# Twelve groups instead of six get their senders by edge number, ScalarE issues the dense stores, and results follow 13 steps behind instead of 17

## The chip, the cores and the metric

One core of a Trainium2 chip runs the whole kernel. The metric is the device time of one execution in microseconds (us). TensorE (PE), VectorE (DVE), ScalarE (ACT), GpSimd (POOL) and SyncE (SP) each work through their own instruction list in order and wait on semaphores; DMAs are issued from SP, POOL and, after the change, ACT. Work on SP is only the issuing of DMAs.

## The reference, cut to what matters

```python
# x: 100000 x 128, E = 25000 edges; edge_index = stack([src, dst]), so src is the receiver
recv, send = (edge_index[0], edge_index[1])
f = concatenate([h[recv], h[send], rel_pos, distance], -1)      # 25000 x 260
s = silu(silu(f @ W1 + b1) @ W2 + b2) @ W3 + b3                 # one score per edge
p = exp(s - segment_max(s, recv)[recv])
alpha = p / (segment_sum(p, recv)[recv] + EPS)
msg = h[send] @ Wv * (alpha * node_weight[send])[:, None]
out = layernorm(x + (h + segment_sum(msg, recv)))               # over 128 features
```

Every one of the 100000 rows is normalized; only rows that receive an edge also get a sum of messages.

## The kernel before, in words

The edges are first sorted by receiver (VectorE, up to about 110 us). From there two kinds of work run side by side.

**Dense work.** The 100000 rows are cut into 98 blocks of 1024 (128 partitions by 8 rows). A block is loaded into one of `X_RING` = 8 places of `xin` (`load_block`, line 323), gets its statistics on DVE (`dense_stats`, line 969), a chain of 11 small DVE instructions for four blocks at once turns them into scale and bias (`drs`, up to line 951), and it is scaled in place: 7 of its 8 rows by ACT (`norm`, line 510), one by DVE (`dense_norm`, line 990). SP stores it (`store_block`, line 332). The place is free for block j+8 when that store has landed. The statistics of blocks 2i and 2i+1 belong to turn i, and their scaling to turn i+2.

**Edge work.** The sorted edges make 49 groups of 512. For each group POOL gathers the receivers' rows (`hk`, four indirect DMAs of 128 rows) and the senders' rows (`rec`, four more). The numbers of the senders and the edge features must be brought into sorted order first. For 43 groups this is a *lookup*: one-hot rows on DVE, 24 products on PE (`look`, line 713), a selection on DVE (`take_places`), and four small products (`words`, line 700). For the other six groups (`TAKEN`: 4, 12, ..., 44) POOL gathers number and features from HBM by edge number (`rt`, four indirect DMAs a group, issued ahead of the first `rec`). POOL's list is: `hk` of four groups, all `rt`, then `rec` of group g and `hk` of group g+4 in turn, the last `rec` groups alone, `hk` of groups 39 to 48 (their place in SBUF holds the lookups' tables until then), and at last the scatters of the 49 groups' results (line 447). The scatters begin when SP has seen the last dense store land.

A gathered `rec` group is in one of `HS_RING` = 4 places; SP writes it to HBM (`write_rec`, line 347), which frees the place for group g+4 of the ring, and SP loads it later into `region` (`load_rec`, line 353).

**Turns and steps.** All engines follow one list, `TURNS`. A *step* s is one beat of the edge pipeline: transposes of group s, first layer of s-1, second of s-2, scores of s-3, weighted sums of s-10 (`Z_LAG`), their product with Wv one step later, statistics at s-12 (`Y_LAG`) and the scaled results (`res`, ACT line 559) 17 steps behind. Every fourth step holds the softmax of a batch of four groups. A step has three parts. A *turn* i holds lookup i (while there are lookups), dense pair i, and parts of steps: none in turns 0 to 9, one part in each of turns 10 to 42, and from turn 43 a whole step (turn 43 is step 11). There are 67 steps and 99 turns, of which the last dense statistics fall into turn 48.

SP's list in a turn is: store of a block, the load for the next lookup, `write_rec`, the loads of a step (each with a wait: for z, for y, for the weights of two groups before), a load of a block, a store, a load. Where it waits, everything behind it waits. `write_rec` of group g stands in turn looks(g) - 1 + 7, where looks(g) counts the lookups up to g; a group that is `TAKEN` so shares its turn with a neighbour.

Of the kernel before, what the change touches and what calls it, by code (L numbers as in the profile page):

```python
# [12 lines left out]
P = 128  # L13
# [23 lines left out]
Y_LAG, Z_LAG, M_LAG, KROW_LAG = 12, 10, 9, 8  # L37
LAST_STEP = 67
# [6 lines left out]
REC_LAG = 7  # L45
E_FROM = 10
PARTS = 3
FIRST_TAKEN, TAKEN_STEP = 4, 8
# [26 lines left out]
def turn_plan():  # L75

    plan, left, turn = [], [(s, p) for s in range(LAST_STEP) for p in range(PARTS)], 0
    while left:
        now = []
        if E_FROM <= turn < LOOKS:  # L80
            now.append(left.pop(0))
        elif turn >= LOOKS:
            now.append(left.pop(0))
            while left and left[0][0] == now[0][0]:
                now.append(left.pop(0))
        plan.append(now)
        turn += 1
    return plan
# [5 lines left out]
def looks(g):  # L94

    return sum(1 for v in LOOKED if v <= g)

# [16 lines left out]
def gnn_kernel(nc, x, xw, rec5, snd_tab, ef_tab, rcv_nat, id_nat, signs, iota, rowid, colid, word, w16d, w1, b1, w2, b2, w3, b3,  # L114
# [11 lines left out]
    with ExitStack() as ctx:  # L126
# [171 lines left out]
        def chain_turn(b):  # L298
            return batch_end(b) + Y_LAG + 1

        def res_turn(g):
            return max(chain_turn(batch_of(g)) + 1 + g % BATCH, g + Y_LAG + BATCH + 1)
# [3 lines left out]
        def _(sp):  # L306
# [18 lines left out]

            def store_block(j):
                if 0 <= j < NB:
                    wait(sp, "norm_a", j + 1)
                    wait(sp, "norm_d", j + 1)
                    if j == NB - 1:  # L330
                        wait_ring(sp, stored, j - 1, 16)
                    sp.dma_start(out[rows_of(j), :].rearrange("(p r) h -> p r h", p=P), xin[:, j % X_RING]
                                 ).then_inc(stored[j % X_RING], 16)
# [53 lines left out]
            for i, now in enumerate(TURNS):  # L387
                store_block(2 * (i - 3) + 1)
                if i + 1 < LOOKS:
                    load_places(i + 1)  # L390
                for g in range(G):
                    if looks(g) - 1 + REC_LAG == i:
                        write_rec(g)
# [19 lines left out]
                store_block(2 * (i - 2))  # L413
# [89 lines left out]
        def _(act):  # L503
            def norm(i, half):
                j = 2 * (i - 2) + half
                if 0 <= j < NB:
                    wait(act, "chain_d", (j // 4 + 1) * STEPS)
                    for n in range(ACT_ROWS):
# [17 lines left out]
            def hidden(s):  # L526
# [7 lines left out]
                for b in range(NBATCH):  # L534
                    if batch_end(b) + 4 == s:
# [4 lines left out]
            def results(s):  # L540
                g = s - Z_LAG
# [4 lines left out]
                for b in range(NBATCH):  # L546
                    if batch_end(b) + 5 == s:
                        n = group_tiles(b)
                        wait(act, "alphaT_done", b + 1)
                        wait(act, "acol_ready", b - 1)  # L550
                        nc.scalar.activation(alT[:, b % 2, 0:n], bank[6][:, 0:n], ACT.Copy).then_inc(S["alT_ready"], 1)
# [27 lines left out]
        def _(pe):  # L579
# [79 lines left out]
            def small_turns(s):  # L659
# [6 lines left out]
                for b in range(NBATCH):  # L666
                    if batch_end(b) + 5 == s:
# [23 lines left out]
            def turns(s):  # L691
                if s + 1 < G:
                    turn_rows(s + 1)
                    turn_senders(s + 1, sum(batch_end(b) + 5 <= s for b in range(NBATCH)))
# [46 lines left out]
        def _(dve):  # L741
# [220 lines left out]
            def dense_stats(i):  # L962
# [10 lines left out]
                if i % 2 == 1 or i == NPAIR - 1:  # L973
# [3 lines left out]
                    def gate():  # L977
                        wait(dve, "norm_a", 4 * (k - 1))
                        wait(dve, "norm_d", 4 * (k - 1))
# [4 lines left out]
            def dense_norm(i):  # L984
                for j in (2 * (i - 2), 2 * (i - 2) + 1):
                    if 0 <= j < NB:
                        wait(dve, "chain_d", (j // 4 + 1) * STEPS)
                        for n in range(ACT_ROWS, BR):
# [103 lines left out]
            def part_two(s):  # L1092
                for b in range(NBATCH):
                    if chain_turn(b) == s:
                        def gate(b=b):
# [3 lines left out]
                                             "chain_e", b * STEPS, gate))  # L1099
                    if batch_end(b) + 4 == s:  # L1100
                        softmax_first(b)
                    if batch_end(b) + 6 == s:
# [6 lines left out]

            def part_three(s):  # L1110
# [3 lines left out]
                for b in range(NBATCH):  # L1114
                    if batch_end(b) + 4 == s:
                        softmax_second(b)
                more(99)
                if s == batch_end(NBATCH - 1) + 5:
                    dve.sem_inc(S["parts_ready"], 1)

            for i, now in enumerate(TURNS):
# [3 lines left out]
                for b in range(NBATCH):  # L1125
                    if (batch_end(b) + 4, 0) in now:
                        take_scores(b)
# [119 lines left out]
```

## Time and profile before

| | |
|---|---|
| median of 3 runs | 1012.76 us (1011.95 to 1016.06) |
| profiled execution, its time | 1010.98 us |
| its span in the trace | 1009.2 us |
| PE / DVE / ACT / POOL busy | 735.5 / 655.5 / 527.1 / 596.9 us |
| moved by DMA | 188.47 MB |
| lookups on PE | 110.3 to 560.2 us |
| last step on PE | 955 us |
| last scatter issued | 1007.5 us |

The span runs from the first to the last instruction; 1.8 us of the execution's time lie around it. An engine's busy time is a mean over stages that differ: sort (to 110 us), lookups without steps, lookups with a third of a step, whole steps with dense work (to about 663 us), whole steps alone, and an end in which only POOL has much to do.

### The profile page before, as it was taken

Reading aid. Unit: us, or ns where it says so; the run is one execution under the profiler, and the core shown is the slowest. Engines: PE = TensorE matmul, PEld = TensorE weight load, DVE = VectorE, ACT = ScalarE, POOL = GpSimd, SP = SyncE. Lnnn points to the kernel's source line nnn. Section 1 sums busy time; section 2 is a strip of 40 time slices with the busy share of each in tenths; the row PEclk is TensorE's granted clock in tenths of the full one; section 3 lists DMA queues with packets and bytes.
Section 4 is the critical chain, followed back from the end, with each engine's and each line's share of the span. In section 5 each row is a group of like instructions: output and inputs, shape, how many; then the busy total and the mean of one; then the engine's idle time right before and its main releaser. Section 6 shows DMA issues by size and latency. Waiting matters only on the chain.

```text
span 1009.2 us, 13449 instructions
## 1 busy us (share of the span) xinstructions
PE 735.5 (73%) x3718; PEld 493.6 (49%) x3718; DVE 655.5 (65%) x2314; ACT 527.1 (52%) x1230; POOL 596.9 (59%) x624
## 2 busy tenths in 40 slices
PE   0001688889878878797889786799999999996700
PEld 0000355555555545564556454566766666665600
DVE  8988789877766757676787666544355535547741
ACT  0000066566555645555556576876566666664630
POOL 3000777777777777777774337717644444446677
PEclk9999988989987878888898988899999999998755
DMA  6000369999889979979999869533322222222131
GB/s 215 0 0 5 78 186 315 336 344 344 288 269 320 327 217 331 329 223 291 356 321 321 247 208 304 168 117 101 92 80 83 80 83 85 83 65 66 65 80 45
DMA packets 120371, 188.47 MB, mean 187 GB/s; under 512 B 21147, under 2 KB 80182, under 8 KB 120296
## 3 DMA queue, kind: packets, MB, share of 16 engines
q1 hardware_dynamic: 100648, 148.85, 45.5%
q0 software_dynamic: 19648, 38.74, 13.8%
q8 instruction: 31, 0.51, 0.2%
q14 instruction: 44, 0.36, 0.1%
HBM read 109.89 MB, written 77.76 MB: 186 GB/s over the span
## 4 chain that ended last, share of the span: by engine, by line
PE 41%; DVE 19%; POOL 15%; issue 8%; DMA 8%; ACT 6%; SPq 2%; POOLq 0%; DVEq 0%; ACTq 0%
PE bank L713 9%; POOL rec L443 6%; POOL hk L443 6%; PE bank L680 4%; PE bank L687 4%; PE bank L643 4%; PE bank L655 4%; PE bank L634 3%; DMA xin<-in_x 3%; POOL out_rows L447 3%; PE bank L652 3%; PE bank L653 3%; ACT xin L510 3%; DVE region L776 3%; PE bank L700 2%
## 5 line engine op out<-in xcount | busy, mean ns | idle before, releaser
L510 ACT ACTIVATE xin<-xin,drs 128x128 f32<-128x128 f32 x686 | 269.4, 480 | 268.8 <-DVE drs L951 268.8
L447 POOL DMA_INDIRECT out_rows<-hk,sidx_t x196 | 192.4, 982 | 155.6 <-ACT hk L559 83.8
L713 PE MATMUL bank<-hk 128*125 128x512 bf16 x1032 | 267.5, 422 | 8.3 <-DVE snd_i L1026 5.4
L443 POOL DMA_INDIRECT hk<-in_x,kg_t x196 | 186.4, 951 | 143.5 <-DVE kg_t L860 84.0
L443 POOL DMA_INDIRECT rec<-in_xw,snd_i x196 | 185.5, 947 | 96.3 <-issue 56.7
L713 PEld LDWEIGHTS bank<-hk 128*125 128x125 bf16 x1032 | 156.7, 154 | 115.1 <-issue 40.6
L969 DVE BATCH_NORM_STATS2 dst<-xin 128x6 f32<-128x256 f32 x392 | 135.6, 413 | 32.8 <-DMA xin<-in_x 32.5
L1011 DVE TENSOR_SCALAR hk<-hk,rid 128x512 bf16<-128x512 f16 x344 | 110.0, 381 | 0.5 <-DMA hk<-vc_d 0.3
L1078 DVE TENSOR_TENSOR hk<-bank,hk 128x512 f32<-128x512 f32 x49 | 33.6, 687 | 102.1 <-PE bank L680 102.1
L700 PE MATMUL bank<-wsel,hk 125*128 125x5 f32 x344 | 52.4, 276 | 59.1 <-DVE hk L1018 59.1
L700 PEld LDWEIGHTS bank<-wsel,hk 125*128 125x128 f32 x344 | 48.6, 218 | 73.2 <-DVE hk L1018 71.7
L559 ACT ACTIVATE hk<-hk,ers 128x128 f32<-128x128 f32 x196 | 79.5, 482 | 0.4 <-DVE ers L951 0.4
L530 ACT ACTIVATE x<-bank,bcol 128x512 f32<-128x512 f32 x49 | 33.6, 686 | 66.5 <-PE bank L655 66.5
L586 PE MATMUL bank<-ident,region 128*128 128x128 f32 x8 | 2.7, 445 | 86.8 <-DVEq L792 86.8
L655 PEld LDWEIGHTS bank<-efT,w 16*128 16x128 f32 x392 | 47.2, 186 | 37.2 <-issue 37.2
L680 PE MATMUL bank<-wvh,zs 128*128 128x128 f32 x392 | 59.6, 300 | 6.8 <-ACT zs L545 3.4
L545 ACT ACTIVATE zs<-bank 128x512 f32<-128x512 f32 x49 | 29.0, 591 | 64.7 <-PE bank L687 64.7
L1069 DVE TENSOR_SCALAR m_q<-krow,kcol,acol 128x128 f32<-128x128 bf16 x196 | 57.1, 348 | 7.4 <-DMA krow<-seg_d 6.4
L1018 DVE SCALAR_TENSOR_TENSOR hk<-hk,cid,bank 125x512 f32<-125x512 f16 x43 | 31.9, 742 | 44.7 <-PE bank L713 44.7
L643 PE MATMUL bank<-x,w2s 128*128 128x512 f32 x98 | 60.9, 706 | 0.0
L687 PE MATMUL bank<-m_q,region 128*128 128x128 f32 x392 | 57.8, 296 | 0.0
L680 PEld LDWEIGHTS bank<-wvh,zs 128*128 128x128 f32 x392 | 52.6, 208 | 9.6 <-ACT zs L545 6.0
(203 smaller groups left out, 1020.7 us busy)
## 6 DMA issues: line engine op xcount, KB each, us to landing
xin<-in_x SPq DMA_DIRECT2D x98, 512.0 KB, 6.8
out_rows<-xin SPq DMA_DIRECT2D x98, 512.0 KB, 7.5
rec_d<-rec SPq DMA_DIRECT2D x49, 258.0 KB, 5.6
region<-rec_d SPq DMA_DIRECT2D x49, 258.0 KB, 3.4
hk<-vc_d SPq DMA_DIRECT2D x43, 256.0 KB
krow<-seg_d SPq DMA_DIRECT2D x49, 128.0 KB, 3.3
hk<-in_x,kg_t POOLq DMA_INDIRECT x196, 5.5
rec<-in_xw,snd_i POOLq DMA_INDIRECT x196, 6.0
```

What stands on the lines that cost most here:

```text
L443: pool.indirect_dma_start(out=to, out_offset=None, in_=frm, in_offset=bass.IndirectOffsetOnAxis(ap=index, axis=0)).then_inc(done, 16)
L447: pool.indirect_dma_start(out=out, out_offset=bass.IndirectOffsetOnAxis(ap=index, axis=0), in_=frm, in_offset=None).then_inc(done, 16)
L510: ins = nc.scalar.activation(xin[:, j % X_RING, n, :], xin[:, j % X_RING, n, :], ACT.Identity, bias=drs[:, j // 4 % 2, 1, c:c + 1], scale= ...
L559: ins = nc.scalar.activation(hk[:, g, q, :], hk[:, g, q, :], ACT.Identity, scale=ers[:, b % 2, 0, n:n + 1], bias=ers[:, b % 2, 1, n:n + 1])
L643: pe.matmul(bank[2][:], w2s[:], x1[:], start=True, stop=True).then_inc(S["mm2_done"], 1)
L655: ins = pe.matmul(bank[1][:, q * P:(q + 1) * P], w16[:, q, :], efT[:, g % 2, :], start=False, stop=(q == TPG - 1), skip_group_check=True)
L680: ins = pe.matmul(bank[4][:, q * P:(q + 1) * P], zs[:, q * P:(q + 1) * P], wvh[:], start=True, stop=True)
L687: ins = pe.matmul(bank[5][:, q * P:(q + 1) * P], rr[:, g % R_RING, q, 0:H], m_q[:, g % 2, q, :], start=True, stop=True)
L700: ins = pe.matmul(bank[7][:, q * WORDS:(q + 1) * WORDS], sel[0:SEL, q * P:(q + 1) * P], wsel[0:SEL, :], start=True, stop=True)
L713: ins = pe.matmul(bank[7][0:SEL, :], tab[:, k, n, 0:SEL], oh[:, k, :], start=(k == 0 and n == 0), stop=(k == CH - 1 and n == PIECES - 1))
L969: ins = vec.bn_stats(dst[:, c:c + 2, :].rearrange("p j w -> p (j w)"), xin[:, j % X_RING, n:n + 2, :].rearrange("p j h -> p h j"))
L1011: ins = vec.tensor_scalar(pair(oh[:, k, :]), vt[:, u % 2, :, 0, :], rid[:, k:k + 1], None, ALU.is_equal)
```

## The change

- `TAKEN_STEP` goes from 8 to 4: twelve groups (4, 8, ..., 48) take their numbers by `rt`, and 37 lookups are left.
- `E_FROM` goes from 10 to 11, and while there are lookups every third turn holds two parts: 4/9 of a step a turn. Turn 37 holds the last two parts of step 11, turn 38 is step 12, turn 51 is step 25. There are 60 steps and 86 turns.
- `write_rec` of group g stands in turn g + 9, one in each turn, behind the step's loads and the first block load, and `HS_RING` is 6.
- The stores of the dense blocks go from SP to ACT: one behind `norm(i, 0)`, one behind the step's parts. `norm_d` is waited for only where DVE has a share.
- ACT scales all 8 rows of a block in turns before 37 (`act_rows`), 5 of 8 after; DVE the other 3.
- The lags: sums 8 steps behind, weights 7, statistics 10, results 13; softmax one step earlier, and its transposed weights are copied and used within one step.

```diff
-HS_RING, R_RING, X_RING = 4, 12, 8
+HS_RING, R_RING, X_RING = 6, 12, 8
-ACT_ROWS = 7
-Y_LAG, Z_LAG, M_LAG, KROW_LAG = 12, 10, 9, 8
-LAST_STEP = 67
+Y_LAG, Z_LAG, M_LAG, KROW_LAG = 10, 8, 7, 6
+LAST_STEP = 60
-REC_LAG = 7
-E_FROM = 10
+REC_LAG = 9
+E_FROM = 11
-FIRST_TAKEN, TAKEN_STEP = 4, 8
+FIRST_TAKEN, TAKEN_STEP = 4, 4
...
         if E_FROM <= turn < LOOKS:
             now.append(left.pop(0))
+            if (turn - E_FROM) % PARTS == PARTS - 1:
+                now.append(left.pop(0))
...
+def act_rows(j):
+    return BR if j // 2 + 2 < LOOKS else 5
...
+            return batch_end(b) + Y_LAG
-            return max(chain_turn(batch_of(g)) + 1 + g % BATCH, g + Y_LAG + BATCH + 1)
+            return chain_turn(batch_of(g)) + (g % BATCH if batch_of(g) < NBATCH - 2 else 0)
...
-                store_block(2 * (i - 3) + 1)
-                for g in range(G):
-                    if looks(g) - 1 + REC_LAG == i:
-                        write_rec(g)
...
-                store_block(2 * (i - 2))
+                if 0 <= i - REC_LAG < G:
+                    write_rec(i - REC_LAG)
...
+            def store(j):
+                if 0 <= j < NB:
+                    wait(act, "norm_a", j + 1)
+                    wait(act, "norm_d", shared(j))
+                    if j == NB - 1:
+                        wait_ring(act, stored, j - 1, 16)
+                    act.dma_start(out[rows_of(j), :].rearrange("(p r) h -> p r h", p=P), xin[:, j % X_RING]
+                                  ).then_inc(stored[j % X_RING], 16)
...
                 norm(i, 0)
+                store(2 * (i - 3) + 1)
                 for s, part in now:
                     (turned, hidden, results)[part](s)
+                store(2 * (i - 2))
                 norm(i, 1)
```

**POOL, around its first `rec` gather** (`rt` are the numbers by edge number, each row a run of indirect DMAs). Before:

```order
13 L443 DMA hk<-in_x,kg_t 128x128 x16
14 L443 DMA rt<-in_rec,idx_t 128x5 x24
15 L443 DMA rec<-in_xw,snd_i 128x129 x4
16 L443 DMA hk<-in_x,kg_t 128x128 x4
17 L443 DMA rec<-in_xw,snd_i 128x129 x4
```

After:

```order
13 L442 DMA hk<-in_x,kg_t 128x128 x16
14 L442 DMA rt<-in_rec,idx_t 128x5 x48
15 L442 DMA rec<-in_xw,snd_i 128x129 x4
16 L442 DMA hk<-in_x,kg_t 128x128 x4
17 L442 DMA rec<-in_xw,snd_i 128x129 x4
```

Twenty-four more gathers stand ahead of the first senders' rows; the rest of POOL's list is as it was.

**SP, at the write-back of group 42** (`out_rows<-xin` is a dense store, `rec_d<-rec` a write-back, `region<-rec_d`, `yf_d`, `yl_d` and `krow` are a step's loads and stores, `far` and `cont` those of a softmax). Before, from the write-back of group 42 (turn 44) to those of 43 and 44 (turn 45):

```order
291 L347 DMA rec_d<-rec 128x4x129
292 L353 DMA region<-rec_d 128x4x129
293 L377 DMA krow<-seg_d 128x512
294 L360 DMA far<-far_d 16x129
295 L361 DMA cont<-cont_d 16x128
296 L323 DMA xin<-in_x 128x1024
297 L332 DMA out_rows<-xin 128x1024
298 L323 DMA xin<-in_x 128x1024
299 L332 DMA out_rows<-xin 128x1024
300 L347 DMA rec_d<-rec 128x4x129 x2
```

After, from the write-back of group 41 (turn 50) to that of group 42 (turn 51):

```order
270 L349 DMA rec_d<-rec 128x4x129
271 L355 DMA region<-rec_d 128x4x129
272 L386 DMA yf_d<-hk 1x512
273 L386 DMA yl_d<-hk 1x512
274 L379 DMA krow<-seg_d 128x512
275 L349 DMA rec_d<-rec 128x4x129
```

The stores are gone from SP, there is one write-back a turn, and that of group 42 has moved from turn 44 to turn 51, behind the loads of step 25.

**ACT, in the lookups with parts of steps** (`xin` are the rows of dense blocks, the others belong to the step's parts). Before:

```order
72 L510 ACTIVATE xin<-xin,drs 128x128 x14
73 L530 ACTIVATE x<-bank,bcol 128x512
74 L533 ACTIVATE efT<-bank 16x128
75 L510 ACTIVATE xin<-xin,drs 128x128 x28
76 L518 ACTIVATE hkT<-bank 128x512
```

After:

```order
58 L509 ACTIVATE xin<-xin,drs 128x128 x16
59 L568 DMA out_rows<-xin 128x1024
60 L529 ACTIVATE x<-bank,bcol 128x512
61 L532 ACTIVATE efT<-bank 16x128
62 L568 DMA out_rows<-xin 128x1024
63 L509 ACTIVATE xin<-xin,drs 128x128 x16
64 L568 DMA out_rows<-xin 128x1024
```

Each run of scaled rows is longer by a seventh, and two stores a turn now stand in ACT's list.

## Rows read from the trace of the kernel before

**Rows 1.** Stretches (us): length, busy time by engine, PE clock, DMA share, GB/s.
```profile
208.20:295.80 87.60, 76.81 (x352) 49.50 (x353) 65.83 (x228) 53.78 (x134) 66.27 (x71) 0.90 0.95 320
560.20:641.00 80.80, 56.89 (x302) 39.52 (x302) 55.10 (x191) 51.84 (x119) 41.73 (x44) 0.83 0.78 230
641.00:905.00 264.00, 251.28 (x1495) 174.66 (x1494) 122.13 (x404) 177.26 (x376) 134.41 (x137) 0.99 0.33 95
```

**Rows 2.** Timeline of PE, the products of lookups 0, 9, 19 and 42.
```profile
110.31 8.00 PE L713 MATMUL bank<-hk 128*125 128x512 bf16 x24 [2.74 <-DVE hk L1011]
192.01 5.39 PE L713 MATMUL bank<-hk 128*125 128x512 bf16 x24 [0.34 <-DVE snd_i L1026]
290.49 5.34 PE L713 MATMUL bank<-hk 128*125 128x512 bf16 x24
553.83 6.41 PE L713 MATMUL bank<-hk 128*125 128x512 bf16 x24
```

**Rows 3.** Timeline of POOL: start, length, indirect DMA, idle before it.
```profile
119.82 0.94 POOL L443 DMA_INDIRECT rt<-in_rec,idx_t  x1 [0.30 <-issue]
149.81 0.95 POOL L443 DMA_INDIRECT rec<-in_xw,snd_i  x1 [0.30 <-issue]
500.60 0.94 POOL L443 DMA_INDIRECT rec<-in_xw,snd_i  x1 [0.30 <-issue]
607.18 1.02 POOL L443 DMA_INDIRECT hk<-in_x,kg_t  x1 [0.31 <-issue]
677.83 1.00 POOL L447 DMA_INDIRECT out_rows<-hk,sidx_t  x1 [20.83 <-SPq L419]
1005.24 1.00 POOL L451 DMA_INDIRECT out_rows<-xin,fixi  x1 [0.30 <-issue]
```

**Rows 4.** Page, part 5: the scatters of the results.
```profile
L447 POOL DMA_INDIRECT out_rows<-hk,sidx_t x196 | 192.4, 982 | 155.6 <-ACT hk L559 83.8
```

**Rows 5.** Waits of SP's own queue over the whole span.
```profile
SPq L347 <- DMA rec<-in_xw,snd_i: 132.1, 31, 8.6
SPq L332 <- ACT xin L510: 61.7, 25, 10.5
```

**Rows 6.** Timelines of SP and of POOL, from 573 us.
```profile
573.27 0.43 SPq L347 DMA_DIRECT2D rec_d<-rec  x1
591.68 1.39 SPq L347 DMA_DIRECT2D rec_d<-rec  x2
...
578.98 0.94 POOL L443 DMA_INDIRECT rec<-in_xw,snd_i  x1 [9.09 <-DMA rec_d<-rec]
597.16 0.94 POOL L443 DMA_INDIRECT rec<-in_xw,snd_i  x1 [13.50 <-DMA rec_d<-rec]
```

**Rows 7.** Timelines of DVE and of SP, blocks 24 to 33.
```profile
223.75 2.40 DVE L969 BATCH_NORM_STATS2 dst<-xin 128x6 f32<-128x256 f32 x7
260.98 2.75 DVE L969 BATCH_NORM_STATS2 dst<-xin 128x6 f32<-128x256 f32 x8
...
246.07 0.34 SPq L332 DMA_DIRECT2D out_rows<-xin  x1
253.23 0.33 SPq L323 DMA_DIRECT2D xin<-in_x  x1
```

**Rows 8.** Line 332, the dense store: ns per issue, least/median/most.
```profile
L332 SPq DMA_DIRECT2D out_rows<-xin x98: 337/394/1785, 131.2 to 663.2; - x98
```

**Rows 9.** Groups of ACT from 560.2 to 641 us, and one timeline row.
```profile
L510 ACT ACTIVATE xin<-xin,drs 128x128 f32<-128x128 f32 x76 | 30.0, 481 | 9.2 <-DVE drs L951 9.2
...
906.13 1.64 ACT L559 ACTIVATE hk<-hk,ers 128x128 f32<-128x128 f32 x4
```

**Rows 10.** Timeline of PE: the sums of groups 11 and 38.
```profile
683.02 1.06 PE L687 MATMUL bank<-m_q,region 128*128 128x128 f32 x8
...
903.87 1.67 PE L687 MATMUL bank<-m_q,region 128*128 128x128 f32 x8
```

**Rows 11.** Timeline of ACT after a step with a softmax.
```profile
627.81 2.42 ACT L510 ACTIVATE xin<-xin,drs 128x128 f32<-128x128 f32 x6 [4.71 <-DVE drs L951]
```

More of the change, by code:

```diff
@@ L96, in looks, with shared @@
     return sum(1 for v in LOOKED if v <= g)
+def act_rows(j):
+    return BR if j // 2 + 2 < LOOKS else 5
+def shared(j):
+    return sum(1 for k in range(j + 1) if act_rows(k) < BR)
 def pool_plan():
@@ L298, in chain_turn @@
         def chain_turn(b):
-            return batch_end(b) + Y_LAG + 1
+            return batch_end(b) + Y_LAG
         def res_turn(g):
-            return max(chain_turn(batch_of(g)) + 1 + g % BATCH, g + Y_LAG + BATCH + 1)
+            return chain_turn(batch_of(g)) + (g % BATCH if batch_of(g) < NBATCH - 2 else 0)
         @block.sync
@@ L324, in load_block @@
                                  ).then_inc(x_in[j % X_RING], 16)
[L326 to L333, printed above, removed]
             for j in range(X_RING):
@@ L507, in norm @@
                     wait(act, "chain_d", (j // 4 + 1) * STEPS)
-                    for n in range(ACT_ROWS):
+                    for n in range(act_rows(j)):
                         c = j % 4 * BR + n
@@ L534, in hidden @@
                 for b in range(NBATCH):
-                    if batch_end(b) + 4 == s:
+                    if batch_end(b) + 3 == s:
                         n = group_tiles(b)
@@ L540, in results @@
             def results(s):
+                for b in range(NBATCH):
+                    if batch_end(b) + 4 == s:
+                        n = group_tiles(b)
+                        wait(act, "alphaT_done", b + 1)
+                        wait(act, "acol_ready", b - 1)
+                        nc.scalar.activation(alT[:, b % 2, 0:n], bank[6][:, 0:n], ACT.Copy).then_inc(S["alT_ready"], 1)
                 g = s - Z_LAG
@@ L545, in results @@
                     nc.scalar.activation(zs[:], bank[5][:], ACT.Copy).then_inc(S["zs_ready"], 1)
[L546 to L551, printed above, removed]
                 for g in range(G):
@@ L666, in small_turns @@
                 for b in range(NBATCH):
-                    if batch_end(b) + 5 == s:
+                    if batch_end(b) + 4 == s:
                         n = group_tiles(b)
@@ L693, in turns @@
                     turn_rows(s + 1)
-                    turn_senders(s + 1, sum(batch_end(b) + 5 <= s for b in range(NBATCH)))
+                    turn_senders(s + 1, sum(batch_end(b) + 4 <= s for b in range(NBATCH)))
             def words(u):
@@ L978, in gate @@
                         wait(dve, "norm_a", 4 * (k - 1))
-                        wait(dve, "norm_d", 4 * (k - 1))
+                        wait(dve, "norm_d", shared(4 * (k - 1) - 1))
                     n = (2 * i + 2 - 4 * k) * BR
@@ L985, in dense_norm @@
                 for j in (2 * (i - 2), 2 * (i - 2) + 1):
-                    if 0 <= j < NB:
+                    if 0 <= j < NB and act_rows(j) < BR:
                         wait(dve, "chain_d", (j // 4 + 1) * STEPS)
-                        for n in range(ACT_ROWS, BR):
+                        for n in range(act_rows(j), BR):
                             c = j % 4 * BR + n
@@ L1099, in part_two, with part_three @@
                                              "chain_e", b * STEPS, gate))
+                    if batch_end(b) + 3 == s:
+                        take_scores(b)
+                        softmax_first(b)
+            def part_three(s):
+                for b in range(NBATCH):
                     if batch_end(b) + 4 == s:
-                        softmax_first(b)
-                    if batch_end(b) + 6 == s:
                         wait(dve, "alT_ready", b + 1)
@@ L1108, in part_two @@
                         dve.wait_ge(S["acol_ready"], b + 1)
-            def part_three(s):
                 if 0 <= s - M_LAG < G:
@@ L1114, in part_three @@
                 for b in range(NBATCH):
-                    if batch_end(b) + 4 == s:
+                    if batch_end(b) + 3 == s:
                         softmax_second(b)
                 more(99)
-                if s == batch_end(NBATCH - 1) + 5:
+                if s == batch_end(NBATCH - 1) + 3:
                     dve.sem_inc(S["parts_ready"], 1)
@@ L1124, in _ @@
                 one_hot(i, 0, EARLY)
-                for b in range(NBATCH):
-                    if (batch_end(b) + 4, 0) in now:
-                        take_scores(b)
                 if 0 <= i - 1 < LOOKS:
```

## The prediction

> **What bounds the kernel now.** I first cut the span at PE's lookups. A lookup's 24 products stand in one row; a turn begins where the products of the lookup before end. Lookup 0 ends at 118.3 us, lookup 9 at 197.4, lookup 19 at 295.8, lookup 42 at 560.2 [rows 2]. So turns 1 to 9 take 8.79 us each (79.1 / 9), turns 10 to 42 11.0 us, of these the first ten 9.84 and the last 23 11.5 (264.4 / 23). The same work gets slower from about turn 20. POOL says why: it issues an indirect DMA every 1.25 us (24 `rt` gathers from 119.82 to 149.81), so that `rec` of g and `hk` of g+4 take 10.02 us together: group 35 starts at 500.60, (500.60 - 149.81) / 35 [rows 3]. 49 groups fall on 43 lookup turns, and 10.02 x 49 / 43 = 11.4 us a turn. SP carries this to the others: its largest wait but one is that of `write_rec` for POOL's gather, 132.1 us, and behind it stand the dense loads [rows 5]. So turns 20 to 42 go at POOL's pace. Those before are held elsewhere: DMA is 95% busy at 320 GB/s and PE 76.8 of 87.6 us [rows 1].
>
> From 560.2 to 641 us six turns hold a whole step and dense work, 13.5 us each, though PE is busy 56.9 of 80.8 us [rows 1]: ACT waits for `drs`, which DVE finishes late behind a softmax (4.7 us at 627.81 [rows 11]), and SP's stores wait for ACT (61.7 us in all [rows 5]). Then come whole steps alone: sums of group 11 at 683.02, of group 38 at 903.87, 8.18 us a step (220.85 / 27) [rows 10], PE 95% busy at a granted clock of 0.99 [rows 1]. At the end POOL scatters: (982 + 300) ns an issue with the gap, 5.13 us a group [rows 4]. The last scatter but the fix-up's two is over by 1005.24 [rows 3].
>
> **The change part by part.** I follow what must happen first for that end.
>
> *Start of the lookups.* Turn 10 loses its part of a step: turn 11 begins at 197.4 + 8.8 = 206.2. Twenty-four more `rt` gathers delay POOL's first `rec` by 24 x 1.25 = 30 us to 179.8. Its write-back stands in turn 9, which begins at 192, so this is just covered: four gathers take 5.0 us, and with a landing of 5.7 us (from 573.27 to 578.98 the write-back lands and frees its place [rows 6]; I take a gather's like it) SP has group 0 at 190.5. Without the move of `write_rec` by two turns it would cost most of the 30.
>
> *Turns 11 to 36.* There are 26. POOL now asks for 190.5 + 10.02(i - 9) at turn i, 461 at turn 36, so its pace is a bound of 10.0 us a turn and no more 11.4. A part more every third turn adds 1/9 of a step on PE: 9.84 + 8.18 / 9 = 10.75 from the ten turns that POOL didn't bound. The second estimate is the ring of `xin`: statistics of block 25 from about 224.7 (the second half of a run that ends at 226.15), store of 25 at 246.07, load of 33 into its place at 253.23, its statistics inside the run from 260.98 to 263.73, whose second half begins at 262.3 [rows 7]. Store to use is 16.2 us, statistics to store 21.4; four turns are 37.6, so t = 9.4, and the 21.4 are two turns and 2.6. After, that store stands behind eight scaled rows of the next turn on ACT (0.39 us each, 30.0 / 76 [rows 9]) and an issue: 3.5 us later, so 2t = 16.2 + 2.6 + 3.5 and t = 11.2. With a longer turn, transfers have less company. I take 10.9, between the two: 206.2 + 26 x 10.9 = 489.6 for turn 37, against 560.2 for turn 43 before. Both are step 11.
>
> *ACT's new work here.* 16 rows x 0.39, two stores at a median of 0.39 and at most 1.79 us [rows 8], and 4/9 of 3.6 us for a step ((51.84 - 30.0) / 6 [rows 1, 9]) make 6.2 + 0.8 + 1.6 = 8.6 us, under 10.9. I cost it at nothing beyond the ring; if a store costs 1.79 each time, it is 11.4, and this half us a turn is the high end. The single scaled row that leaves DVE is worth nothing, as DVE is busy 65.8 of 87.6 us [rows 1].
>
> *Turns 37 to 48*, whole steps and dense work. ACT has 10 x 0.39 for blocks, 3.6 for the step, 1.64 for a result [rows 9], and stores of 0.8: 9.9 us. That is the low end. The high end is 13.5, as now. The stall behind the softmax should shrink: it now falls in even turns, and `drs` is made at the end of odd ones; but the copy of the transposed weights, for which DVE waits in mid-step, now falls in odd ones. SP's loads no longer stand behind ACT. I take 11.6, near the middle: 489.6 + 139.2 = 628.8. Turns 49 and 50 have only ACT's scaling left, 10.8 and 8.1 by the spacing I take from a dense turn and a plain step (my estimate): 647.7 for turn 51.
>
> *From turn 51 to the end.* Here lies the price. POOL's `rec` of group 48 needs the place of group 42 (ring of six), and that write-back stands in turn 51, behind step 25's loads, which wait for step 24. Before, group 48 needed that of 44, in turn 45. Behind `rec` 48 stand ten `hk` groups and all scatters. So: landing 5.7 [rows 6], `rec` 48 5.0, ten `hk` 50.0, 49 scatters 251.3, last scatter to the end 4.0 (1009.2 - 1005.24): 316.0 us. The end of the span is 963.7.
>
> *The short lag* is hidden. Step 49 starts at 647.7 + 24 x 8.18 = 844; result 36 comes about 8 us into it, and 13 groups more take 66.7, then 4.0: 923. POOL is 41 us later. The 20 us that four steps' less lag and 5.13 a group would give are not seen, and the last steps' softmax waits are covered by the same 41 us.
>
> Sum: 1009.2 - 963.7 = 45.5 us off the span. With the 1.8 us around it, 965.5, against 1010.98 for the same execution; the median of the runs shown is another 1.8 above, so 967.
>
> **A rule weighed.** SP's stores waited 61.7 us for ACT's scaling, and those waits held back the loads behind them [rows 5]. The price of the dense turns by that row is my 11.6. The Trainium skill, "DMA: Bandwidth & Descriptors", section "Issuing engines are not separate DMA queues", says that issuing from several engines saves only the sequencer's issue time, usually small beside the transfer. By that rule alone the dense turns would stay at 13.5, and the time would be 990.
>
> **The rivals.**
> - *Forecast, 0.58*: the late write-back of group 42 sets POOL's end; 950 to 982.
> - *The dense turns stay as they are, 0.20.* For it: ACT and DVE still wait for each other once in two turns, and the weights' copy now sits where `drs` is made. Against: SP's waits go. 12 x 1.9 = 22.8 us more: 990.
> - *Both stages reach their floors, 0.12*: 10.0 and 9.9 a turn: 206.2 + 260 + 118.8 + 18.9 + 316.0 + 3.6 = 923.5; half of this way is 945. Against: DMA was 95% busy at 9.8 us a turn.
> - *The write-back doesn't bind and the lag pays, 0.04*: if POOL got through `rec` 48 without waiting, the end is PE's: 923 + 3.6 = 927. Against: the order of SP's list.
> - *ACT's queue becomes the pacer, 0.06*, the case on the other side. A store's issue blocks ACT, and the scaling and the step's copies stand behind it. Stores took up to 1.79 us on SP [rows 8]. From turn 11 to 48 ACT issues 76; the forecast is lost when each costs 45.8 / 76 = 0.6 us more than the 0.39 on the path, 1.0 us; at 1.79 throughout it is 1.4 x 76 = 106 us, 1073. At 1.1 us, 1021. Against: the median.
>
> **How the numbers follow.** 967 is the likeliest. All costs at their high ends (11.4 and 13.5 a turn) give 206.2 + 296.4 + 162 + 18.9 + 316.0 + 3.6 = 1003, all at their low ends 923. Eight times in ten I want the forecast, the unchanged dense turns and half of the way to the floors: 938 to 995. A measurement of this kernel tells about 0.5% from no change. Faster needs less than 1007.7: all but the ACT case, 0.94; within 0.5% 0.02, slower 0.04.
>
> **What would show it.** In the changed kernel's trace: the first `rec` gather at 180 us; turn 37 (after lookup 36) near 490, turns of 10.9; SP's wait for POOL's gathers well under 132 us; POOL idle for a write-back between groups 42 and 48 by some 6 us each, `rec` 48 right behind the write-back of 42 near 648; `hk` 39 near 658, scatters from 709 in one run without waits for ACT; PE's last step some 75 us ahead of the end. Wrong it would be if scatters wait for results, if turns 11 to 36 take over 11.4 us, or if ACT's stores take over 1 us.

## The result and the profile after

The changed kernel takes 935.3 us (median of 4 runs, 929.7 to 942.7) against 1014.4 for the kernel before beside it: a ratio of 0.922, with a 95% interval of 0.915 to 0.930. Forecast were 967 us and a range of 938 to 995, so the direction was right and the time lies 2.7 us outside the range. A second set of runs of the changed kernel, beside the later experiments, gave 935.6 us, ratio 0.923 (0.917 to 0.929); one of its executions, a slow one, took 1431 us; it stands alone among all of them and is not in the ratio.

The profiled execution took 932.8 us; its span is 931.0. First three stretches of the kernel after, in the columns of [rows 1]: the lookup turns 11 to 20, the lookup turns 21 to 36, and turns 37 to 50.

```profile
205.70:302.20 96.50, 83.89 (x424) 55.04 (x422) 71.14 (x245) 70.20 (x174) 73.03 (x78) 0.96 1.01 332
302.20:472.40 170.20, 156.14 (x772) 102.87 (x771) 127.02 (x437) 126.36 (x306) 129.01 (x136) 0.93 0.99 323
472.40:621.90 149.50, 123.49 (x660) 90.15 (x658) 121.04 (x429) 115.44 (x270) 95.13 (x100) 0.89 0.92 283
```

PE's timeline gives the marks of [rows 2]: the products of lookups 9 and 36, and the first products of step 25 (turn 51).

```profile
187.11 5.39 PE L723 MATMUL bank<-hk 128*125 128x512 bf16 x24 [0.34 <-DVE snd_i L1036]
...
465.68 6.69 PE L723 MATMUL bank<-hk 128*125 128x512 bf16 x24
...
621.94 1.05 PE L644 MATMUL bank<-x,wz 128*16 128x128 f32 x8
```

Lookup 36 ends at 472.4 us; 205.7 is where lookup 10 ended, so turns 11 to 36 take 10.26 us each. Before, step 11 followed lookup 42 at 560.2 [rows 2]: PE is 88 us earlier in the same step (of which one part of three already lies behind it).

POOL's timeline answers to [rows 3]: the first `rec` gather, the first issues of group 47's and of group 48's, the first `hk` of group 39, the first scatter, the fix-up's.

```profile
179.79 0.99 POOL L442 DMA_INDIRECT rec<-in_xw,snd_i  x1 [0.30 <-DVE snd_i L1036]
...
615.72 0.94 POOL L442 DMA_INDIRECT rec<-in_xw,snd_i  x1 [8.07 <-issue]
...
620.72 0.94 POOL L442 DMA_INDIRECT rec<-in_xw,snd_i  x1 [0.30 <-issue]
...
625.73 0.94 POOL L442 DMA_INDIRECT hk<-in_x,kg_t  x1 [0.31 <-issue]
...
675.85 1.00 POOL L446 DMA_INDIRECT out_rows<-hk,sidx_t  x1 [0.30 <-issue]
...
927.00 0.99 POOL L450 DMA_INDIRECT out_rows<-xin,fixi  x1 [0.30 <-issue]
```

SP's timeline has the write-backs of groups 41 and 42, which free the places for groups 47 and 48; the page's part 5 has the scatters, as in [rows 4], and the lookups' products:

```profile
611.21 0.42 SPq L349 DMA_DIRECT2D rec_d<-rec  x1
...
614.24 0.47 SPq L349 DMA_DIRECT2D rec_d<-rec  x1
```

```profile
L446 POOL DMA_INDIRECT out_rows<-hk,sidx_t x196 | 191.4, 977 | 59.8 <-issue 58.8
L723 PE MATMUL bank<-hk 128*125 128x512 bf16 x888 | 215.2, 403 | 7.6 <-DVE snd_i L1036 4.7
```

From 614.2 to 620.7, then without a gap to 675.9 and 927.0, and 4.0 us to the end: 316.8 us, where the forecast had 316.0. The scatters wait for little but their own issue (0.9 us of the 59.8 are put down to ACT). But the POOL rows show which place was missing: before group 47, POOL stood idle for 8.07 us, and it began 4.5 us after the write-back of group 41 was issued; group 48 followed with the usual 0.30, since the write-back of group 42 landed at 619.9, while group 47 was still being issued. So it was the write-back of group 41, in turn 50, that POOL waited for in this trace; that of group 42 was 0.8 us from doing the same.

This is also the account of the gain. The scatters start at 675.9 us, and started at 677.8 before [rows 3]: POOL's list has hardly moved. Before, they took 327.4 us (1005.24 - 677.83), since they waited 83.8 us for ACT's results [rows 4]; now they take 251.1. Those 76.3 us and the 1.9 at their start are the 78.2 us by which the span fell. PE gained more than that. In ACT's timeline result 36 stood at 937.0 us before (first row), and stands at 825.4 now:

```profile
936.98 1.64 ACT L559 ACTIVATE hk<-hk,ers 128x128 f32<-128x128 f32 x4
...
825.42 1.64 ACT L558 ACTIVATE hk<-hk,ers 128x128 f32<-128x128 f32 x4
```

What it gained beyond the 78 us is slack: the scatter of group 36 is issued at 860.5.

### The profile page after: what moved, and what is told of

Same layout as the page of the kernel before. It is cut to its first block, busy times and chain, and to the rows that moved or that the text cites. A ratio compares the mean times of both kernels' runs of the same rounds, so it can differ in the third digit from the quotient of the medians.

```text
span 931.0 us, 12940 instructions
## 1 busy us (share of the span) xinstructions
PE 670.7 (72%) x3526; PEld 460.4 (49%) x3526; DVE 629.7 (68%) x2246; ACT 533.7 (57%) x1244; POOL 620.3 (67%) x648
## 3 DMA queue, kind: packets, MB, share of 16 engines
q10 hardware_dynamic: 14112, 51.39, 14.5%
## 4 chain that ended last, share of the span: by engine, by line
PE 38%; POOL 21%; DVE 17%; issue 10%; ACT 9%; DMA 4%; ACTq 0%; SPq 0%; POOLq 0%; DVEq 0%
POOL hk L442 6%; PE bank L723 6%; POOL out_rows L446 5%; POOL rt L442 5%; PE bank L690 5%; POOL rec L442 5%; PE bank L697 5%; ACT xin L509 4%; PE bank L653 4%; PE bank L665 4%; PE bank L644 3%; PE bank L663 3%; PE bank L662 3%; DVE region L786 3%; ACT hk L558 2%
## 5 line engine op out<-in xcount | busy, mean ns | idle before, releaser
L509 ACT ACTIVATE xin<-xin,drs 128x128 f32<-128x128 f32 x700 | 276.1, 480 | 197.2 <-DVE drs L961 190.6
L446 POOL DMA_INDIRECT out_rows<-hk,sidx_t x196 | 191.4, 977 | 59.8 <-issue 58.8
L723 PE MATMUL bank<-hk 128*125 128x512 bf16 x888 | 215.2, 403 | 7.6 <-DVE snd_i L1036 4.7
L723 PEld LDWEIGHTS bank<-hk 128*125 128x125 bf16 x888 | 127.8, 146 | 88.2 <-issue 21.4
L979 DVE BATCH_NORM_STATS2 dst<-xin 128x6 f32<-128x256 f32 x392 | 135.1, 411 | 11.3 <-DMA xin<-in_x 11.2
L1021 DVE TENSOR_SCALAR hk<-hk,rid 128x512 bf16<-128x512 f16 x296 | 92.7, 375 | 0.1
L710 PE MATMUL bank<-wsel,hk 125*128 125x5 f32 x296 | 41.9, 266 | 34.4 <-DVE hk L1028 34.4
L690 PE MATMUL bank<-wvh,zs 128*128 128x128 f32 x392 | 61.7, 307 | 4.7 <-ACT zs L550 2.7
L697 PE MATMUL bank<-m_q,region 128*128 128x128 f32 x392 | 62.5, 313 | 0.0
L710 PEld LDWEIGHTS bank<-wsel,hk 125*128 125x128 f32 x296 | 38.9, 205 | 45.8 <-DVE hk L1028 45.0
L697 PEld LDWEIGHTS bank<-m_q,region 128*128 128x128 f32 x392 | 58.2, 228 | 0.1
L1028 DVE SCALAR_TENSOR_TENSOR hk<-hk,cid,bank 125x512 f32<-125x512 f16 x37 | 27.5, 742 | 44.0 <-PE bank L723 43.9
## 6 DMA issues: line engine op xcount, KB each, us to landing
hk<-vc_d SPq DMA_DIRECT2D x37, 256.0 KB, 6.1
```

The costliest lines, as they stand in the source:

```text
L446: pool.indirect_dma_start(out=out, out_offset=bass.IndirectOffsetOnAxis(ap=index, axis=0), in_=frm, in_offset=None).then_inc(done, 16)
L690: ins = pe.matmul(bank[4][:, q * P:(q + 1) * P], zs[:, q * P:(q + 1) * P], wvh[:], start=True, stop=True)
L697: ins = pe.matmul(bank[5][:, q * P:(q + 1) * P], rr[:, g % R_RING, q, 0:H], m_q[:, g % 2, q, :], start=True, stop=True)
L710: ins = pe.matmul(bank[7][:, q * WORDS:(q + 1) * WORDS], sel[0:SEL, q * P:(q + 1) * P], wsel[0:SEL, :], start=True, stop=True)
L723: ins = pe.matmul(bank[7][0:SEL, :], tab[:, k, n, 0:SEL], oh[:, k, :], start=(k == 0 and n == 0), stop=(k == CH - 1 and n == PIECES - 1))
L979: ins = vec.bn_stats(dst[:, c:c + 2, :].rearrange("p j w -> p (j w)"), xin[:, j % X_RING, n:n + 2, :].rearrange("p j h -> p h j"))
```

## The experiments

All edits are to the changed kernel unless it is said otherwise. Times are medians; ratios are to the kernel before, with their 95% interval. Where a run has no interval, it is one execution. "Lookup 36 ends" and the write-back of group 42 are read from each trace; in the two profiled executions of the changed kernel they are 472.4 and 470.4 us, and 614.2 and 613.1 us.

**Group 42 written back earlier.**

```diff
+def write_turn(g):
+    return min(g + REC_LAG, 45 + (g - 36) // 2) if g >= 36 else g + REC_LAG
...
-                if 0 <= i - REC_LAG < G:
-                    write_rec(i - REC_LAG)
+                for g in range(G):
+                    if write_turn(g) == i:
+                        write_rec(g)
```

> The changed kernel with one edit: from group 36 on two write-backs a turn, so that group 42 is written in turn 48 and not 51. In the changed kernel that write-back was issued at 614.2 us and that of turn 48 at 589.9. If POOL's list behind it sets the end, the end moves with it: 22 to 26 us less than the changed kernel (about 908), up to the point where PE's results set the end (result 36 at 829.7 us plus 13 groups of 5.13 and 4 us = 900). If the end is set elsewhere (PE's last steps), nothing changes.

Measured: 924.5 us, ratio 0.911 (0.907 to 0.915). The scatters start at 670.6 us in this trace, and the span is 925.7: the end moved with them, but by 5 us and not 24. (By the medians the gain is 10.8 us; the traced execution is the slowest of the four, and its lookups ended 7 us late, at 479.6.) SP and POOL in this kernel:

```profile
595.34 0.99 SPq L354 DMA_DIRECT2D rec_d<-rec  x2
...
605.32 0.95 POOL L448 DMA_INDIRECT rec<-in_xw,snd_i  x1 [6.27 <-DMA rec_d<-rec]
```

Groups 40 and 41 go out at 595.3, 42 and 43 at 600.7. The place of group 40 is free 10 us later (POOL waits 6.27 us for it), and groups 46, 47 and 48 then need 5 us each, so 48 starts at 615.3. I had looked at group 42's write-back alone; the ring hands out its places one by one, and with pairs of write-backs that of group 40 became the late one, as that of group 41 was in the changed kernel.

**POOL's list mixed.** The same chain, from its other end:

```diff
+MIX_FROM = 41
...
+    rest = list(range(HK_LOW, G))
     for g in range(G):
         order.append(("hs", g))
         if g + LEAD < HK_LOW:
             order.append(("hk", g + LEAD))
-    order += [("hk", g) for g in range(HK_LOW, G)]
+        elif g >= MIX_FROM:
+            order += [("hk", rest.pop(0)) for _ in range(2) if rest]
+    order += [("hk", g) for g in rest]
...
                 if kind == "hk":
+                    if g == HK_LOW:
+                        pool.wait_ge(S["pay_ready"], LOOKS)
```

> The changed kernel with POOL's list alone altered: from group 41 on the receivers' gathers of groups 39 to 48 stand between the senders' gathers, two groups behind each, and not behind the last. POOL then has 90 us of gathers from 562 us and no wait for a place: scatters begin at 652 instead of 675.9. If POOL's list sets the end, 24 us less than the changed kernel (about 908); if not, no change. The same from another side as the earlier write-backs.

Measured: 911.1 us, ratio 0.898 (0.894 to 0.902), span 907.3. The first scatter in this kernel:

```profile
651.89 1.00 POOL L450 DMA_INDIRECT out_rows<-hk,sidx_t  x1 [0.30 <-issue]
```

At 651.9 us, 24.0 before the changed kernel's, and the span is 23.7 shorter, with lookup 36 at 473.5 and group 42's write-back at 615.7, both where they were. So POOL's list sets the end. This version is 2.6% faster than the changed kernel (0.898 / 0.922) and beats both. Little is left in this way: result 36 is issued at 828.4 and done at 830.0, its scatter stands at 836.3, and for group 39 only 3.1 us lie between the two.

**Results 17 steps behind again.**

```diff
-LAST_STEP = 60
+LAST_STEP = 64
...
-            return chain_turn(batch_of(g)) + (g % BATCH if batch_of(g) < NBATCH - 2 else 0)
+            return chain_turn(batch_of(g)) + 4 + (g % BATCH if batch_of(g) < NBATCH - 2 else 0)
```

> The changed kernel with the results 17 steps behind again, as before the change, all else kept (64 steps). If the shorter lag is hidden behind POOL, as the prediction has it: no change (within 3 us). If scatters wait for results: four steps of 8 us less five of POOL, 20 us more at least.

Measured: 929.0 us, ratio 0.916 (0.911 to 0.920), not slower. The scatters' row still shows no wait for ACT (59.8 us idle, 59.5 of it issue). Result 36 comes at 841.9 instead of 825.4, and its scatter at 856.2. The short lag of the results is hidden.

**SP's wait for a gathered group two turns later**, with the first run's write-backs.

```diff
-    return min(g + REC_LAG, 45 + (g - 36) // 2) if g >= 36 else g + REC_LAG
+    return min(g + REC_LAG, 45 + (g - 36) // 2) if g >= 36 else g + REC_LAG + (g >= 5) + (g >= 10)
```

> As the first run of this call, and in the lookups SP's wait for a gathered group is put two turns later (from group 10 on). If the lookup turns go at POOL's pace through that wait (10.0 us a turn), they get shorter, towards 9.7, and lookup 36 ends near 458 us instead of 472; the end comes earlier only as far as write-backs do. If the ring of dense blocks or PE holds them, the lookups end where they did.

Measured: 931.5 us, ratio 0.918 (0.911 to 0.926). Lookup 36 ends at 476.5. SP's wait for POOL's gathers is 25.5 us instead of 40.1, and the lookup turns did not get shorter: 476.5 lies within the spread of this mark, 470.4 to 479.6 in kernels that are the same up to it. It is not that wait alone. The time of this kernel and of the four below that build on it says little of the lookups: the edit puts the write-back of group 35 behind those of 36 and 37, POOL waits 8.5 us for it before group 41 (issued from 586.5 here), and from there it runs without a gap to the scatters.

**Stores back on SP**: `store` as it was in SP's list, nothing on ACT.

```diff
             for i, now in enumerate(TURNS):
+                store(2 * (i - 3) + 1)
                 if i + 1 < LOOKS:
                     load_places(i + 1)
...
                     write_rec(i - REC_LAG)
+                store(2 * (i - 2))
```

> The changed kernel with the dense stores back in SP's list, in the places that they had before; all else kept. If SP's waits for ACT's scaling are what moving the stores took away, turns 37 to 48 go from 11.0 us back to 13.5 and the end comes up to 25 us later. By the rule of the Trainium skill that was weighed (issuing from another engine saves only issue time), no change beyond 1 us a turn, part of it hidden.

Measured: 944.9 us, ratio 0.931 (0.927 to 0.935), 9.6 us more than the changed kernel by the medians and 12 by the profiled spans (943.0 and 931.0); each of its four executions is slower than each of the seven of the changed kernel that count. Of this kernel SP's wait at its stores, SP's write-back of group 42, and PE's first products of step 25:

```profile
SPq L343 <- ACT xin L520: 117.0, 42, 9.6
```

```profile
626.27 0.43 SPq L358 DMA_DIRECT2D rec_d<-rec  x1
...
620.50 1.05 PE L644 MATMUL bank<-x,wz 128*16 128x128 f32 x8
```

SP waits 117 us for ACT at its stores, yet PE's steps 12 to 22 take 10.85 us each, as in the changed kernel (119.3 and 119.4 us for eleven), and step 25 starts at 620.5 against 621.9. What is late is SP itself: it issues group 42's write-back 5.8 us after step 25 has begun, where with the stores on ACT it was 7.7 us before. POOL waits 6.4 us for that write-back before group 48, and the end follows.

Why the turns don't care is in SP's waits. In the changed kernel, from 472 to 615 us:

```profile
SPq L334 <- DMA out_rows<-xin: 80.7, 21, 7.4
```

This is the load of a dense block waiting for the store that frees its place, and that store now stands in ACT's list. With the stores on SP, the same stretch has 71.2 us of waits for ACT at the stores and 6.6 at the loads. SP's loads still stand behind ACT, for about as long, only through the ring. What changes is the time after the last load, in turn 48: with the stores gone nothing of ACT's stands before the write-backs of groups 41 and 42. So my theory of the dense turns falls, and what the Trainium skill says ("DMA: Bandwidth & Descriptors", section "Issuing engines are not separate DMA queues"), that starting DMAs from several engines saves only the time to start them, agrees with PE's turns, which are 10.85 and 10.86 us; the 12 us at the end come from what else stands in the list that waits, of which that sentence says nothing.

**Six groups taken, 43 lookups.**

```diff
-FIRST_TAKEN, TAKEN_STEP = 4, 4
+FIRST_TAKEN, TAKEN_STEP = 4, 8
```

> The changed kernel with six groups taken by edge number again (43 lookups), all else kept: 4/9 of a step a turn up to turn 42, one write-back a turn, stores on ACT. The write-back of group 42 stays in turn 51, and turns 37 to 42 are lookup turns (10.3 us) instead of whole steps (11.0): by POOL's list the end moves by less than 5 us either way. But step 25 is then in turn 54 and not 51, so PE's results come three steps later, 24 us, and the end by them is about 925 to 935. If the fewer lookups are themselves the gain (as my prediction had it, 6 turns of 10 us), 50 us or more are lost.

Measured: 940.0 us, ratio 0.924 (0.918 to 0.929); the changed kernel's is 0.922, so nothing that these runs can tell. In its trace step 25 starts at 659.8 instead of 621.9 (lookup 42 ends at 539.6), the write-back of 42 is issued at 625.7, and the scatters, from 686.5, still wait for no result (59.8 us idle, 58.5 of it issue). The six lookups fewer make PE 38 us earlier at step 25, and nearly all of it is slack.

**Half of each dense store left out.** Four of eight rows aren't written:

```diff
-                    act.dma_start(out[rows_of(j), :].rearrange("(p r) h -> p r h", p=P), xin[:, j % X_RING]
+                    act.dma_start(out[rows_of(j), :].rearrange("(p r) h -> p r h", p=P)[:, 0:BR // 2, :], xin[:, j % X_RING, 0:BR // 2, :]
```

> The changed kernel, leaving out half of every dense store: four of a block's eight rows are not written, 25 MB less. If the DMA engines (99% busy at 323 GB/s) hold the lookup turns 11 to 36 at 10.3 us, they fall to some 9.5 or less, and lookup 36 ends near 450 us instead of 472. If PE holds them (156 of 170 us busy), lookup 36 ends within 5 us of 472.

Measured: 929.5 us, ratio 0.916 (0.911 to 0.921). Lookup 36 ends at 467.3, 3 to 5 us early: DMA is not what holds the turns alone.

**The third bf16 piece left out**: `for n in range(2)` in `look`, 16 products.

> The changed kernel, leaving out the third of the three bf16 pieces in the lookups: 16 products a lookup instead of 24, so the edge features come with fewer bits. 8 products are 1.7 us at 0.216 us each. If PE holds the lookup turns, turns 11 to 36 fall by that, to 8.6 us, and lookup 36 ends near 428 us; POOL's list then sets the pace (10.0), so rather near 460. If DMA holds them, lookup 36 ends where it did, within 5 us of 472.

Measured: 929.9 us, ratio 0.915 (0.911 to 0.919). Lookup 36 ends at 471.2. SP's wait for POOL's gathers went from 40.1 to 85.4 us. Of this kernel the stretches 205 to 302 and 302 to 470 us, and the group of the products:

```profile
205.00:302.00 97.00, 70.33 (x310) 44.54 (x310) 66.89 (x234) 65.46 (x163) 73.53 (x78) 0.81 0.98 317
302.00:470.00 168.00, 139.20 (x649) 90.93 (x648) 127.97 (x438) 125.28 (x305) 127.16 (x135) 0.86 0.98 325
```

```profile
L723 PE MATMUL bank<-hk 128*125 128x512 bf16 x592 | 165.6, 441 | 7.7 <-DVE snd_i L1036 4.5
```

The granted clock is 0.81 and 0.86 where it was 0.96 and 0.93, and a product takes 441 ns where it took 403 (the group's row above). Part of what PE was spared was lost to the lower clock.

**The write-back's turn and the six places, in the kernel before.**

```diff
-HS_RING, R_RING, X_RING = 4, 12, 8
+HS_RING, R_RING, X_RING = 6, 12, 8
...
-                    if looks(g) - 1 + REC_LAG == i:
+                    if g + 9 == i:
```

> The kernel before with one part of the change alone: write-back of group g in turn g + 9, at its old place in SP's turn, and six places in the ring; six groups taken, stores on SP and all lags as before. If turns 20 to 42 went at POOL's pace through SP's wait (11.5 us), they fall towards the 10.3 us of the changed kernel, lookup 42 ends near 530 us instead of 560, and results come 30 us earlier; scatters, which wait for results, end 25 to 30 us earlier: about 983. If that wait was only slack, no change.

Measured: 983.0 us, ratio 0.969 (0.963 to 0.974), as expected. Lookup 42 ends at 529.4 instead of 560.2, and SP's wait for POOL's gathers, 132.1 us before [rows 5], is gone. This reading of the kernel before, POOL's pace handed on through SP's wait, stands. The turn and the ring were changed together, so their shares are not known. The scatters still wait for results: of this kernel the scatters' group, with 91.1 us idle of which 55.5 are issue.

```profile
L447 POOL DMA_INDIRECT out_rows<-hk,sidx_t x196 | 191.4, 977 | 91.1 <-issue 55.5
```

**Two and more loads relaxed at once**, all on top of the two turns later.

> The kernel of the fourth run (SP's wait for the gathered group two turns later), leaving out half of every dense store: with POOL's pace and the DMA load both relaxed, PE is left. If PE holds the lookup turns, lookup 36 ends at 470 to 477 us as before; if it was DMA or POOL, each hidden by the other when only one was relaxed, near 450.

Measured: lookup 36 ends at 466.6 us (921.3 us in all).

> The kernel of the fourth run (SP's wait for the gathered group two turns later), leaving out the third bf16 piece in the lookups: with POOL's pace and PE both relaxed, DMA is left. If PE held the turns and POOL's pace hid it when only PE was relaxed, lookup 36 ends near 450 us or below; if DMA holds them, at 470 to 477.

Measured: lookup 36 ends at 465.4 us (924.9 in all).

> The kernel of the fourth run (SP's wait for the gathered group two turns later), leaving out half of ACT's scaling while there are lookups: 4 of 8 rows of a block stay unscaled, 3.1 us a turn less on ACT, and both stores of a pair come earlier. If ACT's list (the ring of dense blocks through its stores, or PE's waits for its copies) holds the lookup turns at 10.3 us, lookup 36 ends near 455 us or below; if it doesn't, at 470 to 477.

The edit is `for n in range(4 if act_rows(j) == BR else 5)` in `norm`. Measured: lookup 36 ends at 477.5 us (935.6 in all). So ACT's list is not what holds the lookup turns once POOL's wait is relaxed.

> As the run before, leaving out as well half of every dense store and the third bf16 piece of the lookups: PE, DMA, POOL's pace and ACT are all relaxed at once. If each of them alone is just hidden by the others, the turns fall well under 10 us and lookup 36 ends near 440; if it still ends at 465, something else, the way from DVE's one-hots to PE's words and back, sets the turn.

Measured: lookup 36 ends at 453.9 us (910.3 in all): 9.6 us a turn ((453.9 - 204.5) / 26), between the two outcomes that I had written down.

**The changed kernel again.**

> The changed kernel itself again, beside the others: 928 to 940 us. Its lookup 36 ended at 472.4 us and its group 42 was written back at 614.2; the spread of these marks from one execution to the next tells what differences of a few us in the other runs are worth. The end should again be the start of the scatters and 255 us.

Measured: 935.6 us, as told above. Its scatters start at 676.1, its span is 931.5: 255.4 us, and 255.1 in the first.

**ACT scales 7 rows of 8 after the lookups**, by `else 7` in `act_rows`.

> The changed kernel with ACT scaling 7 of 8 rows of a block in the turns after the lookups, as before the change, and DVE one: 4 rows a turn or 1.6 us more on ACT. If ACT's list sets the turns with a whole step and dense work, steps 12 to 23 go from 10.9 to 12.5 us and the end comes 18 us later; if the place of the softmax set them, by less than 0.5 us a step.

Measured: one execution, 953.2 us, span 951.4. Steps 12 to 22 take 12.2 us instead of 10.9, the write-back of group 42 is issued at 634.0, the scatters start at 696.7. So ACT's list sets most of these turns, and the new split of the rows is worth 18 us of the gain (one execution).

## Why the prediction was right and where it failed

**What bounded the kernel before.** Right for the lookup turns from 20 on: the write-back's turn and two more places in the ring took them, from lookup 20 to 42, from 11.2 us ((560.2 - 312.8) / 22) to 10.1 ((529.4 - 307.8) / 22), and the time to 983 us.

**From turn 51 to the end.** Right as a mechanism, and it is the step on which the forecast stood: a late write-back holds POOL, and POOL's list sets the end. Counted from the write-back of group 42 it is 316.8 us against 316.0, the end lying 255 us (254.6 to 256.0) behind the scatters' start in every trace of the changed kernel and its variants, 24 us less for the whole when POOL's list alone is altered. That the sum held to 0.8 us is in part luck: the place that POOL waited for was that of group 41, and the forecast had it wait for that of 42 as well ("by some 6 us each"), where it waited 8.07 us before group 47 and not before 48. SP issued the two write-backs 3.0 us apart and not a turn apart, for both stood behind one long wait, 11.6 us for DVE's `hk` at the stores of step 24. That the 20 us of the shorter lag would not be seen is shown by the run that gave it back.

**Start of the lookups.** The first `rec` was right, at 179.8. Turn 11 came at 205.7 for 206.2, but by luck in this trace: lookup 9 ended 4.9 us early, at 192.5, and turn 10 took 13.2 us instead of 8.8. In the second trace these are 195.9 and 10.6, and turn 11 comes at 206.5.

What failed is the size of three terms. The 32.7 us between the span that I forecast (963.7) and 931.0 are these three, with 0.5 at the start and 0.8 the other way at the end.

**Turns 11 to 36: 16.7 us.** The step was "I take 10.9, between the two"; 10.26 was measured. The upper of the two, 11.2 from the ring of `xin`, was wrong as put: I added all of the later store's 3.5 us to the way from statistics to store, and kept 16.2 us from store to use. In the trace of the changed kernel the statistics of block 25 begin at 222.3, it is stored at 243.6, block 33 is loaded at 251.2 and its statistics begin at 258.5. From statistics to store that is 21.3 us, no longer than the 21.4 before, and from store to use 14.9. The four turns are 36.2 us: 9.05 us a turn in that stretch, and no bound of 11.2. Whether the ring is a bound at a lower figure isn't shown: no run gives it a ninth place. The lower, 10.75 from PE's added ninth of a step, was not a bound either: the first ten of these turns took 9.65 us ((302.2 - 205.7) / 10), and 9.8 in the second trace, where the kernel before took 9.84 with a third of a step.

What holds them at 10.3 is not one thing. PE is 92% busy in the second stretch, DMA 99%, POOL issues a pair of groups every 10 us. With POOL's wait, DMA or PE relaxed alone, lookup 36 ended at 476.5, 467.3 and 471.2 us; with POOL's wait and one more of DMA, PE and ACT at 466.6, 465.4 and 477.5; with all four at 453.9. But the mark itself spreads: in the five traces whose kernels are the same up to this lookup (the changed kernel twice, the earlier write-backs, POOL's list mixed, ACT with 7 rows) it lies at 472.4, 470.4, 479.6, 473.5 and 472.5. So only the last of these differences, 16.5 us below the lowest of the five, is clear of the spread; with all four relaxed the turn is 0.7 us shorter, and what each is worth isn't shown. What holds the turn at 9.6 then stays open too; DVE's one-hots and the way from them to PE and back are a guess.

**Turns 37 to 50: 8.6 us.** The step was "I take 11.6, near the middle"; steps 12 to 22 took 10.86 us, which is 8.2 us in eleven turns. Turn 37, which holds only two parts, took 7.3 and not 11.6, and against it turns 49 and 50 took 22.9 us and not 18.9. The middle was the wrong choice because the high end, "13.5, as now", rested on SP's stores waiting for ACT, and the run with the stores on SP shows PE's turns unchanged. "SP's loads no longer stand behind ACT" was wrong as well: they waited 80.7 us for ACT's stores to land. ACT's share is what they follow: four rows more made 1.36 us more a turn, near the 1.6 that they cost on ACT. For the other 1.3 us to 13.5 the place of the softmax is my reading, and only argued: with six groups taken the softmax falls in odd turns again, and the steps behind it take 18.4 and 16.9 us, against 14.4 and 13.7 in the changed kernel (14.6 and 14.5 with ACT's larger share).

**SP's place in turn 51: 7.7 us.** The prediction put SP's turn 51 at PE's without a word. With the stores on ACT, SP runs 7.7 us ahead of PE; with them on SP, 5.8 behind. So the stores' move is worth the 12 us between these traces (9.6 by the medians), by another way than the one I gave for it: the late write-back stood behind them. By this sum the time without this term would have been 943, inside the range (an estimate, 935.3 + 7.7).

**The rivals.** "Both stages reach their floors" (923.5, and 945 for half of the way) came nearest to what happened: the stages came to 10.26 and 10.86, over floors of 10.0 and 9.9. By the number alone the 927 of "the write-back doesn't bind" is nearer, but the mixed list shows that it does bind. ACT's queue did not become the pacer: a store's issue took 338 to 391 ns there. The range failed, by 2.7 us, because I kept only half of the way to the floors inside it and had no term for SP's place.

**Where the gain comes from, part by part.** Taken back one at a time, the stores on ACT are worth 10 us, the split of the rows after the lookups 18 (one execution), the six lookups fewer nothing that shows, and the short lag of the results nothing. Added to the kernel before, the write-back's turn and the ring of six are worth 30. The extra part of a step every third turn and the earlier softmax were not taken back alone.

## What to carry to other kernels

Follow the last engine's list backwards to the wait that starts it, and add its own length: that sum held to 1 us, while the stages in front of it were off by several. Look at every place of a ring on that way and not at one: here a neighbour's place was the one waited for. A gain on the engine that looks busiest is worth only what the next chain has spare; here PE came 112 us earlier at result 36 and 78 of them showed. And when a transfer moves to another engine, ask what else stands in the list that it leaves, and whether the wait comes back through a ring.

## What was not expected of the hardware

ACT issued each of its 98 dense stores in 338 to 391 ns while its other work ran; on SP the same issue took 394 ns in the middle and up to 1785 [rows 8], and 468 and up to 1466 with the stores back on SP in the changed kernel. The view of the line in the changed kernel:

```profile
L568 ACTq DMA_DIRECT2D out_rows<-xin x98: 338/338/391, 129.2 to 625.3; - x98
```

With a third of the lookups' products left out, PE's granted clock in the lookups fell from 0.96 to 0.81 and from 0.93 to 0.86, PE being 73% and 83% busy (70.33 of 97, 139.20 of 168) where it was 87% and 92%.
